# Row maxima of two head attentions: one pass per block and a lag of ten waves, or four passes by groups of heads and a lag of four

## The reference, cut to what matters

```python
scores = jnp.einsum('bhqd,bhkd->bhqk', q, k) / jnp.sqrt(jnp.asarray(d, q.dtype))
scores = jnp.where(mask, scores, jnp.asarray(-jnp.inf, q.dtype))
attn = jax.nn.softmax(scores, axis=-1)
return jnp.einsum('bhqk,bhkd->bhqd', attn, v)
```

## Time and profile before

| | us |
|---|---|
| median of three runs | 4437.9 (4435.25 to 4441.99) |
| the profiled execution | 4444.85 |
| its span on the core | 4443.0 |
| mean granted TensorE clock | 0.844 of full speed |
| TensorE matmuls busy | 3420.7 (77%) |
| VectorE busy | 2788.2 (63%) |
| ScalarE busy | 1718.9 (39%) |
| GpSimd busy | 976.4 (22%) |

### The profile page before, as it was taken

The page is one execution under the profiler, slowest core; times in us unless marked ns, Lnnn a source line. Parts: engine busy times, 40 slices in busy tenths (PEclk is TensorE's granted clock), DMA queues, the critical chain, the costliest instruction groups (busy, mean ns, idle before and its releaser), DMA issues. The chain is left out here.

```text
span 4443.0 us, 45602 instructions
## 1 busy us (share of the span) xinstructions
PE 3420.7 (77%) x12125; PEld 1525.2 (34%) x12125; DVE 2788.2 (63%) x4212; ACT 1718.9 (39%) x2599; POOL 976.4 (22%) x516
## 2 busy tenths in 40 slices
PE   5498997799996489877799576766767668767998
PEld 2122224444443144434444222222222234533443
DVE  6867762433345566635433799999999963355444
ACT  2045564244434134443333444545455413312222
POOL 3100000000002100000000476777777720100000
PEclk7569897799998578887899788888888878878999
DMA  4411111000003522210000333333333310000000
GB/s 132 103 34 52 50 40 31 0 0 0 0 24 109 128 60 72 70 49 0 0 0 0 116 124 116 132 116 122 124 124 124 124 55 0 2 0 0 0 0 19
DMA packets 127676, 250.63 MB, mean 56 GB/s; under 512 B 22245, under 2 KB 97658, under 8 KB 110202
## 3 DMA queue, kind: packets, MB, share of 16 engines
q1 hardware_dynamic: 126506, 247.34, 17.0%
q0 software_dynamic: 1024, 1.58, 0.2%
HBM read 191.98 MB, written 56.89 MB: 56 GB/s over the span
## 5 line engine op out<-in xcount | busy, mean ns | idle before, releaser
L1814 POOL TENSOR_TENSOR a_g<-a_g,a_spread 128x1024 f32<-128x1024 f32 x256 | 659.9, 2584 | 576.6 <-DVE a_g L1772 576.6
L1574 PE MATMUL a_y<-a_g,ident 128*128 128x512 f32 x768 | 458.2, 736 | 359.7 <-POOL a_g L1819 216.0
L883 DVE TENSOR_REDUCE a_top<-a_sc 128x1 f32<-128x512 f32 (+3 forms) x1024 | 568.0, 589 | 264.9 <-PE a_sc L772 143.3
L848 ACT ACTIVATE a_prob<-a_st 128x1024 f32<-128x1024 f32 (+2 forms) x512 | 439.2, 865 | 476.1 <-PE a_st L789 294.6
L1772 DVE TENSOR_TENSOR_SCAN a_g<-a_decay,a_drive 128x512 f32<-128x512 f32 x512 | 596.5, 1206 | 0.0
L455 DVE TENSOR_TENSOR f_s<-f_a,f_spread 128x512 f32<-128x512 f32 x392 | 267.9, 687 | 434.8 <-ACT f_a L440 268.8
L769 PE MATMUL a_sc<-a_k,a_q 72*128 72x512 bf16 (+3 forms) x1024 | 402.4, 404 | 138.4 <-DMA a_k<-a_k_rows 63.1
L1694 ACT ACTIVATE a_decay<-a_delta,a_capped_a 128x512 f32<-128x512 f32 x512 | 337.2, 712 | 430.6 <-DVE a_capped_a L1744 235.4
L422 PE MATMUL f_y<-f_s,f_w 128*128 128x512 f32 x784 | 401.3, 599 | 21.1 <-DVE f_s L455 20.4
L415 PE MATMUL f_hid<-h,f_w 128*128 x784 | 404.9, 601 | 6.1 <-PEq L246 6.1
L1574 PEld LDWEIGHTS a_y<-a_g,ident 128*128 128x128 f32 x768 | 163.5, 227 | 629.3 <-issue 401.0
(11 more groups left out here) (323 smaller groups left out, 4688.3 us busy)
## 6 DMA issues: line engine op xcount, KB each, us to landing
a_spread<-a_bc_rows SPq DMA_DIRECT2D x128, 1024.0 KB, 4.6
a_q<-a_q_rows SPq DMA_DIRECT2D x64, 288.0 KB
a_pv_rows<-a_pv_sb SPq DMA_DIRECT2D x64, 256.0 KB, 2.0
a_q_rows<-p_qp SPq DMA_DIRECT2D x72, 128.0 KB
a_q_rows<-a1q_qp SPq DMA_DIRECT2D x72, 128.0 KB
a_k_rows<-a1q_kp SPq DMA_DIRECT2D x72, 128.0 KB
a_k<-a_k_rows SPq DMA_DIRECT2D x32, 288.0 KB
a_k_rows<-p_kp SPq DMA_DIRECT2D x72, 64.0 KB
```

What stands on the lines that cost most here:

```text
L848: nc.scalar.activation(prob[w % 2][:, j, 0:width(kp)], st[:, j % 2, 0:width(kp)], ACT.Exp, scale=a.scale).then_inc(s.exp_done, 1)
L883: nc.vector.tensor_reduce(top[:, t, n:n + 1], sc[:, t % 2, 0:w], AX.X, ALU.max).then_inc(s.maxed, 1)
L1574: last = nc.tensor.matmul(y[:, k, :], S.ident[:, :], g[:, n % 8, k, :], start=(n == 0), stop=False)
L1814: nc.gpsimd.tensor_tensor(g[:, n % 8, :, :], g[:, n % 8, :, :], spread[:, pair % 4, 2 + n % 2:3 + n % 2, :].to_broadcast([P, H2, L]), ALU. ...
```

## The change

- The keys' half runs `BEHIND` = 4 waves behind the scores instead of ten: in waves 0 to 3 of block b it does waves 4 to 7 of block b - 1, in waves 4 to 7 waves 0 to 3 of block b itself. One extra call of the body, of which four waves do something, takes the place of the two.
- The maxima are handled by groups of four heads. When the last of a group's 16 reductions is done, VectorE splits that part of `top` where it is, with tokens on the partitions (four operations on 128 x 16 elements, a chain: `split`). TensorE turns the bf16 parts (four matmuls with 16 columns against the identity, `turn`) in the middle of the next wave, after the third and fourth score tile of the next head have been issued, into slot 0 of `sc`. VectorE copies the 16 x 512 result to a bf16 tile `max_row` (`copy_rows`) after the reductions of that head, and the first score tile of the head after it waits for the copy. The turn of group 3 falls into wave 0 of the next block.
- GpSimd stores and loads back each group by itself: four stores of 12 rows of 512 and four loads of 3 rows of 2048 per block instead of one of each with four times the size. It waits for each store before it issues the load.
- The keys' scores of a group wait for that group's load (`max_loaded` is waited for four times per block).
- SyncE's loads and stores are put in an order that fits the new lag: the loads of block b + 1 begin at the start of block b.

```diff
-        def waves(b, B1, B2):
+        def waves(b, A, B):
             for w in range(8):
-                if w < 2:
-                    yield w, (b - 2 if B1 else None), w + 6, 0
+                if w < BEHIND:
+                    yield w, (b - 1 if B else None), w + 8 - BEHIND, 1
                 else:
-                    yield w, (b - 1 if B2 else None), w - 2, 1
+                    yield w, (b if A else None), w - BEHIND, 0
...
-                pool.wait_ge(s.max_parts, nB + b + 1)
-                alone(pool, S)
-                nc.gpsimd.dma_start(a.max_rows[k].rearrange("i (h n) -> h i n", h=H), max_part[:, :, :]
-                                    ).then_inc(s.max_stored, 16)
-                pool.wait_ge(s.max_stored, 16 * (nB + b) + 16)
-                alone(pool, S)
-                nc.gpsimd.dma_start(q[k][ROWS:ROWS + 3, :, :].rearrange("r h n -> r (h n)"), a.max_rows[k]
-                                    ).then_inc(s.max_loaded[k], 16)
+                for g in range(4):
+                    pool.wait_ge(s.max_copied, 4 * (nB + b) + g + 1)
+                    alone(pool, S)
+                    nc.gpsimd.dma_start(a.max_rows[k, g], max_row[g % 2][0:12, :]).then_inc(s.max_stored, 16)
+                    pool.wait_ge(s.max_stored, 64 * (nB + b) + 16 * g + 16)
+                    alone(pool, S)
+                    nc.gpsimd.dma_start(q[k][ROWS:ROWS + 3, 4 * g:4 * g + 4, :].rearrange("r h n -> r (h n)"),
+                                        a.max_rows[k, g].rearrange("(i h) n -> i (h n)", i=3)).then_inc(s.max_loaded[k], 16)
...
-                if t == 0 and n == 0 and not (isinstance(b, int) and b == 0 and call == 0):
-                    pe.wait_ge(s.max_parts, nB + b)
+                if t == 0 and n % 4 == 1 and not (isinstance(b, int) and b == 0 and call == 0 and n < 4):
+
+                    pe.wait_ge(s.max_copied, 4 * (nB + b) + n // 4)
...
-                if w == 0 and j == 0:
+                if kp == 0 and j == 0:
...
+            def turn(b, g, reduced):
+
+                pe.wait_ge(s.max_parts, 4 * (nB + b) + g + 1)
+                pe.wait_ge(s.maxed, reduced)
+                for t in range(TC):
+                    last = nc.tensor.matmul(sc[0:16, 0, t * P:(t + 1) * P], max_part[:, t, :, :].rearrange("p i h -> p (i h)"),
+                                            S.ident_b[:, :], start=True, stop=True)
+                last.then_inc(s.max_turned, 1)
...
-                if A:
-                    pe.wait_ge(s.maxed, (nB + b) * 64 + 64 + 2)
-                    for t in range(TC):
-                        last = nc.tensor.transpose(sc[0:H, 0, t * P:(t + 1) * P], top[:, t, :], S.ident[:, :])
-                    last.then_inc(s.max_turned, 1)
+                        if j == 1 and w % 2 == 0:
+                            if w > 0 and A:
+                                turn(b, w // 2 - 1, (nB + b) * 64 + 8 * w + 2 + 1 + 2)
+                            elif w == 0 and B:
+                                turn(b - 1, 3, (nB + b) * 64 + (2 + 1 if A else 0) + 2)
...
+            def split(b, g):
+                chain = Chain(dve, s.max_step, 4 * (4 * (nB + b) + g) + call + 1)
+                most = top[:, :, 4 * g:4 * g + 4]
+                dve.wait_ge(s.maxed, (nB + b) * 64 + 16 * g + 16 + 2)
+                chain(nc.vector.tensor_scalar(max_part[:, :, 0, :], most, -1.0, None, ALU.mult))
+                chain(nc.vector.scalar_tensor_tensor(out=max_rest[:, :, :], in0=most, scalar=-1.0,
+                                                     in1=max_part[:, :, 0, :], op0=ALU.mult, op1=ALU.subtract))
+                chain(nc.vector.tensor_copy(max_part[:, :, 1, :], max_rest[:, :, :]))
+                chain(nc.vector.tensor_tensor(max_part[:, :, 2, :], max_rest[:, :, :], max_part[:, :, 1, :], ALU.subtract))
+                dve.sem_inc(s.max_parts, 1)
+
+            def copy_rows(b, g):
+                dve.wait_ge(s.max_turned, 4 * (nB + b) + g + 1)
+                if not (isinstance(b, int) and b == 0 and call == 0 and g < 2):
+                    dve.wait_ge(s.max_stored, 16 * (4 * (nB + b) + g - 1))
+                nc.vector.tensor_copy(max_row[g % 2][:, :], sc[0:16, 0, :]).then_inc(s.max_copied, 1)
...
+                    if n % 4 == 0:
+                        if n > 0:
+                            copy_rows(b, n // 4 - 1)
+                        elif B:
+                            copy_rows(b - 1, 3)
+                    if n % 4 == 3:
+                        split(b, n // 4)
```

More of the change, by code:

```diff
@@ L607, in attend @@
         top = sb("top", [P, TC, H])
-        max_rest = sb("max_rest", [H, L])
-        max_part = sb("max_part", [H, 3, L], BF16)
+        max_rest = sb("max_rest", [P, TC, 4])
+        max_part = sb("max_part", [P, TC, 4, 4], BF16)
+        max_row = [sb(f"max_row{k}", [16, L], BF16) for k in range(2)]
         pv_sb = [sb(f"pv_sb{k}", [P, L]) for k in range(2)]
@@ L674, in load_v, with body @@
                              ).then_inc(s.v_loaded[k], 16)
[L676 to L687, removed]
-                        store(b - 1, g)
[L690 to L694, removed]
+            def body(b, A, B, k):
+                first = isinstance(b, int) and b == 0
+                last = isinstance(b, int) and b == NB - 1
+                if A and not last:
+                    for g in range(2):
+                        load(b + 1, g, 1 - k, first=first)
+                    load_v(b + 1, 1 - k, first=first)
+                for g in range(1, 4):
+                    if B:
+                        store(b - 1, g)
+                    if A and not last and g < 3:
+                        load(b + 1, g + 1, 1 - k, first=first)
+                if A:
+                    store(b, 0)
             for g in range(4):
@@ L698, in _ @@
             load_v(0, 0, first=True)
-            body(0, True, False, False, 0)
-            body(1, True, False, True, 1)
+            body(0, True, False, 0)
+            body(1, True, True, 1)
             with sp.Fori(1, NB // 2 - 1) as i:
                 for k in range(2):
[L704 to L707, removed]
-            for g in range(3):
-                store(NB - 2, g)
-            store(NB - 2, 3)
-            for g in range(4):
-                store(NB - 1, g)
+                    body(2 * i + k, True, True, k)
+            body(NB - 2, True, True, 0)
+            body(NB - 1, True, True, 1)
+            body(NB, False, True, 0)
             for k in range(2):
@@ L810, in products, with body @@
                     last.then_inc(s.pv_done, 1)
-            def body(b, A, B1, B2, k):
-                for w, bb, wb, odd in waves(b, B1, B2):
+            def turn(b, g, reduced):
[5 more added lines that the diff above has]
+                last.then_inc(s.max_turned, 1)
+            def body(b, A, B, k):
+                for w, bb, wb, odd in waves(b, A, B):
                     kb = k ^ odd
@@ L822, in body @@
                             kt = PV_AT.index(j)
-                            if w == 0:
-                                if B1:
-                                    products(b - 2, 5, k, kt)
-                            elif w == 2:
-                                if B1:
-                                    products(b - 2, 7, k, kt)
+                            if w == BEHIND:
+                                if B:
+                                    products(b - 1, 7, k ^ 1, kt)
                             elif bb is not None:
@@ L864, in body @@
                             evacuate(bb, wb // 2 - 1)
-                    if w == 2 and B1:
-                        evacuate(b - 2, 3)
+                    if w == BEHIND and B:
+                        evacuate(b - 1, 3)
             steps(act, body)
```

34 lines of the change are left out of this document (14 added, 20 removed).

## The result

The changed kernel takes **4485.3 us** (median of four runs, 4479.0 to 4490.4) against 4439.9 (4435.3 to 4442.5) for the kernel before on the same chip: a ratio of 1.0103, 95% interval 1.0085 to 1.012. It is 1.0% slower; forecast were 4403 us and 0.8% faster.

A forecast was written before the change was run, and what follows sets the result against it. At full clock VectorE and the two slots of `sc` set the pace. Gains of 14.6 us in layer 0 and 20.6 in layer 1 took the profiled 4444.85 to 4410, or 4403 against the median; range 4376 to 4452.

The forecast's parts named there:

- The stop at a block's end goes: End of each block: VectorE's stop, 4.07 us in layer 0, disappears.
- And with it, by my choice, the low clock: After each block's end: the low clock, 4.4 us per block in layer 0, 5.1 in layer 1, goes too.
- The argument for it: Tail follows the same four VectorE operations at clock 1.00; full-clock waves at 325 to 351 us hold despite TensorE's idles.
- The rival: Clock falls all the same, at TensorE's waits for the copy and at the split: 47 us back, 4450; chance 0.19.
- the 0.9 at the split: 0.9 us at each group's split, named as one place where the clock might fall.
- Products and keys' scores stand on both sides: Around the new pauses TensorE has work, unlike today's block-end stops with hardly any for 3.3 us; argued against clock falls.
- The rule cited from the Trainium skill: Small idles between groups of matmuls suffice to swing TensorE's clock; the forecast held the trace at 325 to 351 us against it.
- Costs per group: Split, copy and wait per four heads: 0.9 + 0.7 + 0.5 = 2.1 us in layer 0, 1.45 in layer 1.
- Tails: Keys-only waves at each attention's end, four instead of ten: 22.3 us in layer 0, 18.1 in layer 1.
- Layer 1: Causal attention: total 425.6 us, gain 20.6, clock 1.00 after warm-up but for two dips after jumps.
- The trip: Maxima through memory by GpSimd: 7.1 us today, some 6 us for a quarter of the bytes; no wait taken.
- The jump in layer 0: Loop's jump back: priced in layer 1 only, 2 x 9.0 = 18.1 us with its low clock; nothing for layer 0.

The follow-up runs named there:

- the late chain: Changed kernel with the split's four operations in one piece before the fourth reduction of the next head instead of the first; 4404.8 us, ratio 0.9892.
- one operation: Changed kernel with the last three of the split's four operations left out (part of the computation missing); 4403.2 us, ratio 0.993.
- both spread ones: Changed kernel with the split's four operations one each before the next head's four reductions, 4398.7 us; the same with the copy on ScalarE, 4381.5 us.
- the lag of six: Changed kernel with the split's operations spread over four reductions and BEHIND = 6 instead of four; 4394.4 us.
- the two with the late chain in layer 0 and a spread one in layer 1: Changed kernel, split before the fourth reduction in layer 0, one operation before each in layer 1: 4394.1 us; same with copy on ScalarE: 4380.3 us.
- the table's row in bold: Changed kernel with split spread over four reductions, copy on ScalarE, and blocks 2 to 7 as straight code without loop; 4332.7 us, ratio 0.9768.
- the spread kernel: Changed kernel with the split's four operations one each before the four reductions of the next head, copy still on VectorE; 4398.7 us, ratio 0.9908.

## Why the prediction was wrong, step by step

- **The stop at a block's end goes: right. "And with it, by my choice, the low clock": wrong in layer 0, and this is the step that failed.** Forecast for the stage 501.5, measured 572.8 us. Low clock after the first 25 us was forecast at some 27 us and came to 227. Two pairs of kernels price it: the changed kernel with and without its loop, which in layer 0 differ in the clock alone, 33.1 us for 85.7 us of low clock, 0.39; the late chain against the changed kernel, 97.7 us less 24 for its shorter pair (14.2 us) for 215, 0.34. So 200 us too many cost 68 to 78 us, about the whole miss of 71. What stood in its place is the standing at the split: the falls went to 2 with the operations spread and to none with the same chain placed late, and stayed (18) with the copy moved.
- **The argument for it had a hole.** The tail and the four waves at full clock have pauses, but none in which VectorE holds both slots while TensorE's queue starts with a score tile. "Products and keys' scores stand on both sides" of the split is true of the order in which they are issued, yet the next products stood behind that score tile: TensorE stood 0.85 us until 238.92.
- **The rival had the right mechanism, and one of its two places was right**: it named "the 0.9 at the split" and, first, TensorE's wait for the copy, which was 0.60 us at most at full clock in the changed kernel's layer 0 and had no fall behind it there. It got a chance of 0.19 and a price of 47 us, today's low time. That was the second mistake: with four splits per block instead of one stop the price is not bound by today's. Layer 0's 71 us above the forecast, nearly all of it the clock, decided the sign.
- **The rule cited from the Trainium skill** (TensorE: Matmul & The Clock Gate, A second HAM failure mode) spoke for that rival. The trace agrees: all fourteen falls stand at or just behind standings of about a microsecond, though ten more such standings brought none. I set the rule aside on the strength of the earlier trace rows, where the pauses lay elsewhere.
- **Costs per group: right.** Small operations 0.17 (0.16 to 0.19), split 0.85 (0.9), copy 0.68 (0.7), wait 0.56 (0.5), turns hidden; the pair 15.01 (14.83) in layer 0 and 12.41 (12.13) in layer 1, the reductions behind two copies there starting at 1627.69 and 1640.10. At full clock, then, a block gains nothing, as said.
- **Tails 23.2 and 16.9 us (22.3 and 18.1): right.**
- **Layer 1: right in kind**, 438.7 (425.6). The clock is 1.00 but for the two jumps. These cost 21.2 us (18.1), the longer pair 8, and keys' scores waited three times for the rows (3.65, 0.88 and 0.24 us), 5 us in all, where the forecast had put no wait.
- **The trip: right in layer 0, not quite in layer 1.** The median store took 1.69 us until the load was issued, not 2.06. In layer 0 nothing waited. In layer 1 eight of the 32 stores took 2.40 to 7.55 us, and the longest, in block 0, made the wait of 3.65 us.
- **The jump in layer 0: missed.** Nothing was put down for it, since the earlier trace rows shows it for TensorE in layer 1 alone. The changed kernel did not pay it, but six variants did (one operation, both spread ones, the lag of six, and the two with the late chain in layer 0 and a spread one in layer 1): about 4 to 6 us twice, and the low clock behind.

How much there was to win shows in the table's row in bold: with the clock at 1.00 the stages are 55 and 57 us shorter than before. At 0.34 to 0.39 per us, the 122 and 119 us of low clock that went make 41 to 48 and 40 to 46 of that; the shorter fill and tail, less the work per group, give only the rest.

## What to carry to other kernels

Where two engines pass tiles through two slots, as here, a pause on the consumer can cost more than its length once TensorE has nothing else at the head of its queue: look for each added operation at what TensorE would issue under it, and put small chained operations one each between large ones, where they cost 0.09 instead of 0.21 us here and made no standing that the clock fell at. Price the clock by its own records (low time and number of falls per stage) and not as a by-product of the one stop that you remove. Then look at the jumps of loops on every engine, since one that is free under a stop, or in one layout of the code, cost 4 to 6 us and a fall of the clock here when it was bare.

## What the runs showed of the hardware that I had not expected

- Standings of TensorE of 0.85 to 1.42 us at a split came with falls of the clock that lasted 3.4 to 37.5 us, fourteen times out of 24 in layer 0 of the changed kernel; waits of up to 0.60 us for the copy, ahead of products, came with none there.
- The same jump costs VectorE nothing in the layer 0 of one kernel and 4.0 us, sometimes 2.1 more, in another whose loop differs by few instructions; TensorE stood 5.16 and 5.22 us at it in layer 1. In straight code of six blocks neither engine had such a stop.
- After the same event in one execution, the jump in layer 0 of the spread kernel, the clock came back once after 6.8 us (fall at 416.4) and once after 41.0 (fall at 535.8).
